# Moving the layer-norm scaling of a four-layer graph network from ScalarE to VectorE, and a rectifier into the copy behind a transpose

## The chip, the cores and the metric

The kernel runs on one core of a Trainium2 chip. The metric is the time of one execution on the device in microseconds (us), as the median of several runs. Everything is computed in float32.

## The reference

Sixty-four batches, each a matrix x of 256 nodes by 128 features, share one adjacency matrix adj (256 x 256). Four layers follow one another, each of the form x = x + f(h), with h the rectified layer norm of x:

```python
h = jnp.maximum(_layernorm(x, axis=-1), 0.0)   # (x - mean) / sqrt(var + 1e-5), before every layer
x = x + layer(h, ...)
# layer 0, W = adj: s1 = h @ adj[:, :128].T, s2 = h @ adj[:, 128:].T
pre = s1[:, :, None, :] + s2[:, None, :, :] + b_lin
h = jnp.where(pre >= 0, pre, ALPHA * pre)       # for all i, j, e
e = jnp.einsum('bije,e->bij', h, a) + bias       # then softmax, attn @ x, sigmoid
# layer 1: dense graph layer with elu, an edge sigmoid and two products
# layer 2: attention with tanh(A / 8) * 8, exp and the adjacency as a mask
# layer 3: five steps of a gated recurrent unit, messages adj @ h
```

Layer 0 holds nearly all of the work: for each batch, 256 x 256 pairs of nodes times 256 values of e go through a leaky rectifier and are summed over e with weights a.

## The kernel before

A turn of the main loop handles a pair of batches; there are 32 pairs and two more turns in which the last pair runs out. A turn has 128 places, called lots, 64 for either batch of the pair. In a lot that is not left out (116 of the 128 from the third turn on, all 128 before it) eight blocks of 128 x 256 values max(u_i, w_j) are made, and TensorE sums them over the partitions into the score bank S with four products (eight records of the trace, L1163). The blocks go into a ring of 12 buffers, so makers can be up to 12 lots ahead of TensorE.

Each block is made by one of three engines. ScalarE does it as a rectifier of a PSUM copy plus a bias (L956, tile ring). GpSimd does it in a tensor-scalar on SBUF (L620). VectorE does it in tensor-tensors of one, two or four blocks (L746, L751), whose w operand lies in PSUM, and in some rows as a max plus a second tile `signed` (L742) that GpSimd makes (L610) and that covers both values of e at once. Which engine gets which block of which lot is settled when the program is built, by the class `Plan`: `stage_costs` books a cost for every other stage of work on its engine near its lot, and `share_blocks` gives the blocks of each lot so that the three running sums of cost stay level. The costs are in units of about 0.1 us: `VECTOR_BLOCK, VECTOR_START, SCALAR_BLOCK, POOL_BLOCK = 2.67, 0.69, 3.57, 4.75`. The stage that makes `src_bias` in layer 1 (L833, four custom instructions on two SBUF operands) is booked as `source=8`.

The other layers run in the same turns, spread over fixed lots by tables: POST is the end of layer 0 of one batch, PRE the layer norm and projections of the next batch (h = 0 or 1), LN1, LN2, LN3 are the norms ahead of layers 1 to 3 of the pair before (four blocks of 128 x 128), L1 and L2 those layers, and L3 the recurrent steps, which go on into the next turn. Every engine runs its own program in order: in each lot first its blocks, then its stages. TensorE does a stage three lots early (LEAD). On VectorE, a stage of several dependent instructions puts one held-back piece of the lot's blocks (`one_piece`) ahead of each wait on its own result; `spare_blocks` says how many pieces are held back.

A layer norm before the change: VectorE takes bn_stats and bn_aggr per block (L802, L808; for PRE L767, L772), then two tiny tensor-scalars, minus_mean (L812, L776) and var + eps (L813, L777). GpSimd raises var to -1/2 (L582) and multiplies minus_mean by it into shift (L584). ScalarE makes the rectified norm with one activation for each block, with scale rstd and bias shift (L1006 for layers 1 to 3, L964 for PRE). TensorE transposes h into PSUM and ScalarE copies it out (L1014, L1041, L1061, L968).

Work on VectorE that reads two SBUF tensors beside GpSimd's: the state update of layer 3 (L890 rh, L894 diff, L898 gated, L902 h3T), the mask products, and L833. In setup_layer0, at the start, L670 multiplies a 128 x 256 SBUF tile by one column in a tensor-scalar.

Of the kernel before, what the change touches and what calls it, by code (L numbers as in the profile page):

```python
# [30 lines left out]
ALU = mybir.AluOpType  # L31
# [3 lines left out]
P = 128  # L35
N = 256
NB = N // P
# [63 lines left out]
class Plan:  # L101
# [45 lines left out]
    def stage_costs(self):  # L147

        vector, scalar, pool = [0.0] * LOTS, [0.0] * LOTS, [0.0] * LOTS

        def put(costs, table, at, **stages):
            for name, cost in stages.items():
                book(costs, at + table[name], cost)

        def book(costs, t, cost):

            costs[t % LOTS] += cost / 2
            costs[(t - AHEAD) % LOTS] += cost / 2

        for h in range(2):  # L160
            half = h * LOTS_B
            if self.turn or h:
                put(vector, POST[h], half, score=7, transpose=1.5, residual=3.4)
                put(scalar, POST[h], half, exp=8, copy=3, tanh=5)
            put(vector, PRE[h], half, stats=7.0)
            put(scalar, PRE[h], half, norm=7.7, copy=2.7, evacuate=32)
            put(pool, PRE[h], half, factors=12)
            if self.has_sums:
                book(pool, half, 11)
        if self.turn:  # L170
            for ln in (LN1, LN2, LN3):
                put(vector, ln, 0, stats=12.5)
                put(scalar, ln, 0, norm=15.4, copy=4.8)
                put(pool, ln, 0, factors=12)
            put(pool, L1, 0, shift=13, halves=13)
            put(vector, L1, 0, elu=10, source=8, mask=12, agg_copy=6, recv_elu=10, residual=6)
            put(scalar, L1, 0, exp=5.7, edge_copy=4.8, tanh=14.2, agg_copy=4.8, recv_exp=5.7)
            put(vector, L2, 0, mask=11.4, residual=11.8)
            put(scalar, L2, 0, copy=9.6, tanh=9.6, exp=9.5)
        for s in range(STEPS):  # L180
            for costs, stages in ((vector, dict(update=7, state=18, out=6 if s == STEPS - 1 else 0)),
                                  (scalar, dict(copy=4.8, reset=5.7, z_gate=5.7, tanh=5.7, back=4.8 if s < STEPS - 1 else 0))):
# [33 lines left out]
    def spare_blocks(self):  # L216

        spare = [0] * LOTS
        for h in range(2):
            for at in (POST[h]["transpose"], PRE[h]["stats"], PRE[h]["stats"]):  # L220
                spare[h * LOTS_B + at] += 1
        for ln in (LN1, LN2, LN3):
            spare[ln["stats"]] += 2
        for at in (L1["elu"], L1["recv_elu"], L2["residual"]):
            spare[at] += 1
        for s in range(STEPS):
            spare[layer3_lot(s, "state")] += 2
        return spare
# [45 lines left out]
def gnn_stack(nc, x, adj, L0_b, L0_a, L1_Wi, L1_bi, L1_We, L1_be, L1_Wn, L1_bn, L1_Wm, L1_bm, L2_q, L2_k, L2_v,  # L274
# [42 lines left out]
    with ExitStack() as ctx:  # L317
# [62 lines left out]
        rstd0 = sb("rstd0", [P, NB])  # L380
        minus_mean0 = sb("minus_mean0", [P, NB])
        shift0 = sb("shift0", [P, NB])
        neg_score = sb("neg_score", [P, NB, N])
# [19 lines left out]
        rstd = sb("rstd", [P, 3, 4])  # L403
        minus_mean = sb("minus_mean", [P, 3, 4])
        shift = sb("shift", [P, 3, 4])
        h1 = sb("h1", [P, 4, P])
# [43 lines left out]

        x_loaded, pre_stats, pre_mv, pre_eps, pre_rstd = (sem(n) for n in "x_loaded pre_stats pre_mv pre_eps pre_rstd".split())
        pre_shift, h0_ready, h0T_psum, h0T_ready = (sem(n) for n in "pre_shift h0_ready h0T_psum h0T_ready".split())
        clamps_ready, signed_ready = sem("clamps_ready"), sem("signed_ready")
# [9 lines left out]
        ln_rstd = [sem(f"ln{n}_rstd") for n in (1, 2, 3)]  # L463
        ln_shift = [sem(f"ln{n}_shift") for n in (1, 2, 3)]
        h_ready = [sem(f"h{n}_ready") for n in (1, 2, 3)]
# [106 lines left out]
        def _(gp):  # L572
# [5 lines left out]

            def factors(var_, minus_mean_, rstd_, shift_, width, sem_in, sem_rstd, sem_shift, value):

                gp.wait_ge(sem_in, value)
                gp.tensor_tensor(rstd_, var_, minus_half[:, 0:width], ALU.pow).then_inc(sem_rstd, 1)  # L582
                gp.wait_ge(sem_rstd, value)
                gp.tensor_tensor(shift_, minus_mean_, rstd_, ALU.mult).then_inc(sem_shift, 1)  # L584

            def pre(value):
                factors(var0[:], minus_mean0[:], rstd0[:], shift0[:], NB, pre_eps, pre_rstd, pre_shift, value)

            def norm(n, turn):
                factors(var[:, n], minus_mean[:, n], rstd[:, n], shift[:, n], 4, ln_eps[n], ln_rstd[n], ln_shift[n], turn.at(1, 0))  # L590

# [64 lines left out]
        def _(dve):  # L656
# [105 lines left out]
            def pre(p, y, value):  # L762

                if p == PRE[1 - y]["stats"]:
# [33 lines left out]

            def stats(t, ln, n, src, pair):
                if t == ln["stats"]:  # L800
# [22 lines left out]
            def layer1(t, turn):  # L823
                pair = turn.at(1, 0)
                if t == LN1["stats"]:
                    dve.wait_ge(x1_ready, turn.at(2, 0))
                stats(t, LN1, 0, X1, pair)
                if t == L1["elu"]:
# [24 lines left out]
            def layer2(t, turn):  # L853
                pair = turn.at(1, 0)
                if t == LN2["stats"]:
                    dve.wait_ge(x2_ready, pair)
                stats(t, LN2, 1, X2, pair)
                if t == L2["mask"]:
# [19 lines left out]
            def layer3(t, turn):  # L878
                if turn.has_l12:
                    if t == LN3["stats"]:  # L880
                        dve.wait_ge(x3_ready, turn.at(1, 0))
                    stats(t, LN3, 2, X3, turn.at(1, 0))
                pair, s, p = layer3_at(turn, t)
# [58 lines left out]
        def _(act):  # L942
# [57 lines left out]

            def norm(t, ln, n, src, dst, pair):

                if t == ln["norm"]:
                    act.wait_ge(ln_shift[n], pair)
                    for r in range(4):
                        last = act.activation(dst[:, r], src[:, r], ACT.Relu, bias=shift[:, n, r:r + 1], scale=rstd[:, n, r:r + 1])  # L1006
                    last.then_inc(h_ready[n], 1)

            def layer1(t, turn):
                pair = turn.at(1, 0)  # L1010
                norm(t, LN1, 0, X1, h1, pair)
# [24 lines left out]
            def layer2(t, turn):  # L1036
                pair = turn.at(1, 0)
                norm(t, LN2, 1, X2, h2, pair)
# [17 lines left out]
            def layer3(t, turn):  # L1056
                if turn.has_l12:
                    norm(t, LN3, 2, X3, h3, turn.at(1, 0))
# [304 lines left out]
```

## Time and profile before

| | |
|---|---|
| median of 3 runs | 5407.69 us (5406.17 to 5408.93) |
| time of the profiled execution | 5412.65 us |
| its span, first to last instruction | 5410.9 us |
| mean granted TensorE clock | 0.996 |
| VectorE busy | 5225.0 us, 97% of the span |
| ScalarE busy | 5143.4 us, 95% |
| GpSimd busy | 5080.7 us, 94% |
| TensorE busy with matmuls | 5288.8 us, 98% |

Busy times are unions of instruction spans, so an instruction that waits inside its span counts as busy. The last 130 us or so are the two turns without layer 0, in which all engines but TensorE are mostly idle.

### The profile page before, as it was taken

The numbers are of one execution on the slowest core, as the hardware profiler recorded it, in microseconds if no ns is written. First come the engines' busy times: TensorE is split into PE (matmuls) and PEld (weight loads), VectorE is DVE, ScalarE is ACT, GpSimd is POOL, SyncE is SP. The second block draws the span as 40 slices with busy tenths as digits, with TensorE's granted clock in tenths as the row PEclk, the third lists the DMA queues.
The fourth block names the chain that finished last, engine by engine and source line by source line (L and its number), as shares of the span: only waits on it lengthen the run. The fifth ranks groups of instructions, "written<-read, shape, count | busy, mean of one in ns | idle before, by whom it ended". The sixth has DMA issues, their size and how long they took to land.

```text
span 5410.9 us, 115261 instructions
## 1 busy us (share of the span) xinstructions
PE 5288.8 (98%) x37702; PEld 2060.9 (38%) x37702; DVE 5225.0 (97%) x10763; ACT 5143.4 (95%) x13517; POOL 5080.7 (94%) x9752
## 2 busy tenths in 40 slices
PE   8999999999999999999999999999999999999997
PEld 2333333333333333333334333333333333333334
DVE  9999999999999999999999999999999999999993
ACT  8999999999999999999999999999999999999993
POOL 8899999999999999999999999999999999999990
PEclk9999999999999999999999999999999999999998
DMA  0000000000000000000000000000000000000000
GB/s 15 3 4 7 7 6 3 6 7 7 6 7 3 6 7 7 6 3 6 7 7 6 7 3 6 7 7 6 3 6 7 7 6 7 3 6 7 7 5 6
DMA packets 44381, 34.00 MB, mean 6 GB/s; under 512 B 4752, under 2 KB 39696, under 8 KB 43792
## 3 DMA queue, kind: packets, MB, share of 16 engines
q1 hardware_dynamic: 43792, 26.63, 1.6%
q8 instruction: 311, 5.10, 0.4%
q14 instruction: 278, 2.28, 0.1%
HBM read 9.84 MB, written 8.39 MB: 3 GB/s over the span
## 4 chain that ended last, share of the span: by engine, by line
PE 52%; ACT 26%; DVE 20%; issue 2%; DMA 0%; POOL 0%; SPq 0%; DVEq 0%; POOLq 0%
PE S L1163 29%; ACT ring L956 20%; PE R L1108 9%; DVE ring L751 8%; PE S L1108 5%; DVE ring L742 4%; PE W L1108 3%; DVE ring L746 2%; PE R L1301 2%; PE V L1108 1%; ACT h L1006 1%; DVE rh L890 1%; DVE gated L898 1%; DVE diff L894 1%; DVE h3T L902 1%
## 5 line engine op out<-in xcount | busy, mean ns | idle before, releaser
L956 ACT ACTIVATE ring<-V,U_minus 128x256 f32<-128x256 f32 x10681 | 4338.4, 850 | 1.6 <-issue 1.6
L1163 PE MATMUL S<-ring,a_window 128*32 128x512 f32 x29888 | 3401.9, 596 | 51.0 <-DVE ring L746 21.4
L620 POOL TENSOR_SCALAR ring<-W,U 128x256 f32<-128x256 f32 x6362 | 3175.7, 518 | 12.1 <-ACT V L982 11.8
L751 DVE TENSOR_TENSOR ring<-U,W 128x512 f32<-128x512 f32 (+1 forms) x2884 | 2536.1, 903 | 7.3 <-ACT V L982 7.3
L1163 PEld LDWEIGHTS S<-ring,a_window 128*32 128x32 f32 x29888 | 886.5, 109 | 2294.5 <-issue 2052.1
L610 POOL TENSOR_SCALAR signed<-W_signed,U_ceiling,U_floor 128x256 f32<-128x256 f32 x2880 | 1699.6, 594 | 6.3
L742 DVE SCALAR_TENSOR_TENSOR ring<-W,U,signed 128x256 f32<-128x256 f32 x2880 | 1193.8, 471 | 0.0
L746 DVE TENSOR_TENSOR ring<-U,W 128x256 f32<-128x256 f32 x1747 | 711.4, 409 | 0.0
L1108 PE MATMUL R<-mT,W 128*128 128x512 f32 (+1 forms) x640 | 334.9, 605 | 16.3 <-ACT mT L1068 16.3
L1108 PE MATMUL R<-AT,h 128*128 128x256 f32 x1264 | 311.9, 390 | 2.1 <-ACT h L1080 2.1
L582 POOL TENSOR_TENSOR rstd<-var,minus_half 128x4 f32<-128x4 f32 (+1 forms) x160 | 144.0, 900 | 141.2 <-DVE var L813 125.6
L1108 PEld LDWEIGHTS R<-AT,h 128*128 128x128 f32 x1264 | 230.6, 193 | 78.4 <-issue 50.3
L890 DVE SCALAR_TENSOR_TENSOR rh<-tr,h3T 128x512 f32<-128x512 f32 (+1 forms) x164 | 165.1, 1007 | 58.3 <-ACT tr L1071 58.3
L1074 ACT ACTIVATE tz<-R,bias 128x512 f32<-128x512 f32 (+1 forms) x160 | 161.1, 1007 | 52.4 <-PE R L1301 52.3
L1006 ACT ACTIVATE h<-X,shift,rstd 128x128 f32<-128x128 f32 x384 | 193.8, 870 | 6.8 <-POOL shift L584 6.8
L1080 ACT ACTIVATE h<-R 128x512 f32<-128x512 f32 (+1 forms) x128 | 131.8, 1029 | 69.5 <-PE R L1309 69.5
L1108 PEld LDWEIGHTS R<-mT,W 128*128 128x128 f32 x640 | 110.5, 192 | 172.0 <-ACT mT L1068 93.7
L1068 ACT ACTIVATE mT<-R 128x512 f32<-128x512 f32 (+1 forms) x160 | 165.0, 1031 | 11.0 <-PE R L1108 11.0
L1301 PE MATMUL R<-mT,W 128*128 128x512 f32 (+1 forms) x320 | 168.5, 608 | 0.0
L1071 ACT ACTIVATE tr<-R,bias 128x512 f32<-128x512 f32 (+1 forms) x160 | 157.6, 985 | 9.6 <-PE R L1108 9.6
L1077 ACT ACTIVATE cand<-R,bias 128x512 f32<-128x512 f32 (+1 forms) x160 | 164.7, 1029 | 0.7 <-PE R L1108 0.7
L1108 PE MATMUL R<-h3T,turned 128*128 128x512 f32 (+1 forms) x320 | 162.6, 590 | 0.0
(185 smaller groups left out, 4512.9 us busy)
## 6 DMA issues: line engine op xcount, KB each, us to landing
X<-in_x SPq DMA_DIRECT2D x64, 128.0 KB, 2.1
X_held<-X SPq DMA_DIRECT2D x32, 256.0 KB, 2.3
out<-OUT SPq DMA_DIRECT2D x64, 128.0 KB, 1.9
edge<-in_L_gnn_w_w SPq DMA_DIRECT2D x3, 128.0 KB, 2.2
A<-in_adj SPq DMA_DIRECT2D x1, 256.0 KB, 2.7
Wn<-in_L_gnn_Wn SPq DMA_DIRECT2D x1, 128.0 KB, 2.9
Wm<-in_L_gnn_Wm SPq DMA_DIRECT2D x1, 128.0 KB, 3.0
weight<-in_L_gnn_u_w SPq DMA_DIRECT2D x2, 64.0 KB, 2.2
```

What stands on the lines that cost most here:

```text
L610: made = gp.tensor_scalar(signed[:, number % 2, at], W_signed[:, y], U_ceiling[:, y, i:i + 1], U_floor[:, y, i:i + 1], ALU.min, ALU.max)
L620: last = gp.tensor_scalar(ring[:, place, g, half * N:(half + 1) * N], W[:, y, c], LARGEST, U[:, y, c, i:i + 1], ALU.min, ALU.max)
L742: piece = dve.scalar_tensor_tensor(ring[:, place, g, half * N:(half + 1) * N], w, U[:, y, c, i:i + 1], signed[:, number % 2, at], ALU.max, ...
L746: piece = dve.tensor_tensor(ring[:, place, g, half * N:(half + 1) * N], U[:, y, c, i:i + 1].to_broadcast([P, N]), w, ALU.max)
L751: piece = dve.tensor_tensor(ring[:, place, g:g + groups].rearrange("p g (h j) -> p g h j", h=NB), u.unsqueeze(3).to_broadcast([P, groups, ...
L890: dve.scalar_tensor_tensor(rh[:, cols_], tr[:, cols_], 1.0, h3T[:, cols_], ALU.add, ALU.mult).then_inc(rh_ready, 1)
L956: last = act.activation(ring[:, place, g, half * N:(half + 1) * N], W_scalar[y][:, c * N:(c + 1) * N], ACT.Relu, bias=U_minus[:, y, c, i:i ...
L1006: last = act.activation(dst[:, r], src[:, r], ACT.Relu, bias=shift[:, n, r:r + 1], scale=rstd[:, n, r:r + 1])
L1068: act.activation(mT[:, cols_], messages[:, cols_], ACT.Copy).then_inc(mT_ready, 1)
L1108: return pe.matmul(dst, lhsT, rhs, start=start, stop=stop)
L1163: last = pe.matmul(S[y][g * ROWS:(g + 1) * ROWS, :], a_window[:, c, ROWS - 1 - row:2 * ROWS - 1 - row], ring[:, place, g], start=False, st ...
L1301: pe.matmul(gates[:, cols_], W345[:, 0], mT[:, cols_], start=False, stop=True, skip_group_check=True).then_inc(z_psum, 1)
```

## The change

VectorE now makes the norm itself: for each 128 x 128 block one tensor-scalar, (x - mean) * rstd, with the mean and rstd as two pointer columns. In PRE (two blocks) and LN3 (four blocks) a second tensor-scalar takes the max with 0 over all blocks at once, behind a wait and a held-back piece. In LN1 and LN2 there is none: the transposes carry signed values, and ScalarE's copy out of PSUM (L1014, L1041) becomes a rectifier. ScalarE's 16 norm activations of a turn go, minus_mean goes from VectorE, the shift product from GpSimd. The norm stands at the same lots as before, on VectorE. The booked costs change, and so the shares of blocks. At the program's start, VectorE waits for rstd and makes the first norm ahead of setup_layer0.

```diff
-            put(vector, PRE[h], half, stats=7.0)
-            put(scalar, PRE[h], half, norm=7.7, copy=2.7, evacuate=32)
-            put(pool, PRE[h], half, factors=12)
+            put(vector, PRE[h], half, stats=6.1, norm=6.6)
+            put(scalar, PRE[h], half, copy=2.7, evacuate=32)
+            put(pool, PRE[h], half, factors=8)
...
-                put(vector, ln, 0, stats=12.5)
-                put(scalar, ln, 0, norm=15.4, copy=4.8)
-                put(pool, ln, 0, factors=12)
+                put(vector, ln, 0, stats=11.3, norm=11.8 if ln is LN3 else 7.9)
+                put(scalar, ln, 0, copy=4.8)
+                put(pool, ln, 0, factors=10)
...
-            for at in (POST[h]["transpose"], PRE[h]["stats"], PRE[h]["stats"]):
+            for at in (POST[h]["transpose"], PRE[h]["stats"], PRE[h]["stats"], PRE[h]["norm"]):
                 spare[h * LOTS_B + at] += 1
         for ln in (LN1, LN2, LN3):
             spare[ln["stats"]] += 2
+        spare[LN3["norm"]] += 1
...
                 gp.tensor_tensor(rstd_, var_, minus_half[:, 0:width], ALU.pow).then_inc(sem_rstd, 1)
-                gp.wait_ge(sem_rstd, value)
-                gp.tensor_tensor(shift_, minus_mean_, rstd_, ALU.mult).then_inc(sem_shift, 1)
...
-                    dve.tensor_scalar(minus_mean0[:], mv0[:, :, 0], -1.0, None, ALU.mult)
                     dve.tensor_scalar(var0[:], mv0[:, :, 1], LN_EPS, None, ALU.add).then_inc(pre_eps, 1)
+                if p == PRE[1 - y]["norm"]:
+                    dve.wait_ge(pre_rstd, value)
+                    for r in range(NB):
+                        last = dve.tensor_scalar(H0[:, y, r], X0[:, y, r], mv0[:, r, 0:1], rstd0[:, r:r + 1], ALU.subtract, ALU.mult)
+                    last.then_inc(pre_scaled, 1)
+                    one_piece()
+                    dve.wait_ge(pre_scaled, value)
+                    dve.tensor_scalar(H0[:, y], H0[:, y], 0.0, None, ALU.max).then_inc(h0_ready, 1)
...
-                    dve.tensor_scalar(minus_mean[:, n], mv[:, n, :, 0], -1.0, None, ALU.mult)
                     dve.tensor_scalar(var[:, n], mv[:, n, :, 1], LN_EPS, None, ALU.add).then_inc(ln_eps[n], 1)
+                if t == ln["norm"]:
+                    dve.wait_ge(ln_rstd[n], pair)
+                    for r in range(4):
+                        last = dve.tensor_scalar(dst[:, r], src[:, r], mv[:, n, r, 0:1], rstd[:, n, r:r + 1], ALU.subtract, ALU.mult)
+                    if n < 2:
+                        last.then_inc(h_ready[n], 1)
+                    else:
+                        last.then_inc(ln3_scaled, 1)
+                        one_piece()
+                        dve.wait_ge(ln3_scaled, pair)
+                        dve.tensor_scalar(dst[:], dst[:], 0.0, None, ALU.max).then_inc(h_ready[n], 1)
...
             dve.memset(minus_half[:], -0.5).then_inc(dve_const, 1)
             pre(PRE[1]["stats"], 0, 1)
+            pre(PRE[1]["norm"], 0, 1)
             setup_layer0()
...
-                if p == PRE[1 - y]["norm"]:
-                    act.wait_ge(pre_shift, value)
-                    for r in range(NB):
-                        last = act.activation(H0[:, y, r], X0[:, y, r], ACT.Relu, bias=shift0[:, r:r + 1], scale=rstd0[:, r:r + 1])
-                    last.then_inc(h0_ready, 1)
...
-                    act.activation(h1T[:], S[1][:], ACT.Copy).then_inc(hT_ready[0], 1)
+                    act.activation(h1T[:], S[1][:], ACT.Relu).then_inc(hT_ready[0], 1)
...
-                    act.activation(h2T[:], W_bank[0][:], ACT.Copy).then_inc(hT_ready[1], 1)
+                    act.activation(h2T[:], W_bank[0][:], ACT.Relu).then_inc(hT_ready[1], 1)
```

## Rows read from the trace of the kernel before

**Rows 1.** The page, its part 1: busy time and share of each engine.

```profile
PE 5288.8 (98%) x37702; PEld 2060.9 (38%) x37702; DVE 5225.0 (97%) x10763; ACT 5143.4 (95%) x13517; POOL 5080.7 (94%) x9752
```

**Rows 2.** Windows: stretch, its length, busy PE, PEld, DVE, ACT, POOL; one steady turn, tail.

```profile
2795.30:2961.00 165.70, 163.55 (x1172) 63.62 (x1171) 163.27 (x337) 160.49 (x425) 160.53 (x307) 1.00 0.02 6
...
5280.00:5411.00 131.00, 94.44 (x334) 62.92 (x334) 44.13 (x114) 46.77 (x94) 7.34 (x8) 0.87 0.02 7
```

**Rows 3.** Chain that ended last, that turn, in order of time: start us, us, what.

```profile
2800.85 0.70 DVE diff L894
...
2835.07 0.36 DVE exp L818
...
2837.76 1.06 PE S L1163 x8
...
2928.48 0.69 ACT tz L1074
...
2931.47 6.56 ACT ring L956 x18
2938.03 1.52 ACT h L1006 x4
```

**Rows 4.** Waits in that turn: who waited for whom, us, times, longest.

```profile
DVE X L850 <- PE S L1108: 1.3, 1, 1.3
...
PE S L1163 <- DVE ring L746: 0.5, 1, 0.5
```

**Rows 5.** Groups by form over the whole span: shapes, count, busy us, mean ns.

```profile
L833 DVE CUSTOM_DVE_ANT_0 exp<-xh,We_src,be 128x128 f32<-128x128 f32 x128 | 71.4, 610 | 2.3 <-ACT xh L1020 2.3
...
L812 DVE TENSOR_SCALAR minus_mean<-mv 128x4 f32<-128x4 f32 x96 | 25.2, 262 | 2.2
```

**Rows 6.** Timeline of the start, VectorE and ScalarE (GpSimd has one short instruction).

```profile
4.93 0.17 DVE L665 TENSOR_SCALAR a_minus<-a_col 128x2 f32<-128x2 f32 x1 [0.68 <-DMA b_col<-in_L_gnn_b_lin]
...
5.48 0.61 DVE L670 TENSOR_SCALAR neg_score<-A,a_abs 128x256 f32<-128x256 f32 x2
...
6.01 0.15 DVE L671 TENSOR_TENSOR b_scaled<-b_col,a_abs 128x2 f32<-128x2 f32 x1
```

**Rows 7.** Timeline of the source stage of layer 1, VectorE and GpSimd, steady turn.

```profile
2844.94 0.70 DVE L833 CUSTOM_DVE_ANT_0 exp<-xh,We_src,be 128x128 f32<-128x128 f32 x1
2845.01 0.49 POOL L620 TENSOR_SCALAR ring<-W,U 128x256 f32<-128x256 f32 x1
...
2847.10 0.87 DVE L742 SCALAR_TENSOR_TENSOR ring<-W,U,signed 128x256 f32<-128x256 f32 x2
```

**Rows 8.** Timeline of the same stage in the tail, first and last of four.

```profile
5299.58 0.35 DVE L833 CUSTOM_DVE_ANT_0 exp<-xh,We_src,be 128x128 f32<-128x128 f32 x1 [2.29 <-ACT xh L1020]
...
5300.67 0.08 DVE L833 DVE_READ_ACCUMULATOR2_ANT src_bias<- 128x1 f32 x1
```

**Rows 9.** Timeline of a layer-3 state update, VectorE and GpSimd, steady turn.

```profile
2801.57 0.91 DVE L898 SCALAR_TENSOR_TENSOR gated<-tz,diff 128x512 f32<-128x512 f32 x1
2801.87 1.03 POOL L610 TENSOR_SCALAR signed<-W_signed,U_ceiling,U_floor 128x256 f32<-128x256 f32 x1
2802.52 0.93 DVE L902 SCALAR_TENSOR_TENSOR h3T<-gated,h3T 128x512 f32<-128x512 f32 x1
...
2834.06 0.68 DVE L902 SCALAR_TENSOR_TENSOR h3T<-gated,h3T 128x512 f32<-128x512 f32 x1
```

**Rows 10.** Timeline around one rh of layer 3, VectorE and GpSimd.

```profile
2822.04 2.74 POOL L620 TENSOR_SCALAR ring<-W,U 128x256 f32<-128x256 f32 x6
2823.37 1.96 DVE L890 SCALAR_TENSOR_TENSOR rh<-tr,h3T 128x512 f32<-128x512 f32 x1
2824.76 1.00 POOL L610 TENSOR_SCALAR signed<-W_signed,U_ceiling,U_floor 128x256 f32<-128x256 f32 x1
```

**Rows 11.** Timeline of the tail: the norm of layer 1 on GpSimd and ScalarE.

```profile
5288.78 0.20 POOL L584 TENSOR_TENSOR shift<-minus_mean,rstd 128x4 f32<-128x4 f32 x1
...
5289.02 1.65 ACT L1006 ACTIVATE h<-X,shift,rstd 128x128 f32<-128x128 f32 x4 [1.60 <-POOL shift L584]
```

More of the change, by code:

```diff
@@ L380, in gnn_stack @@
         rstd0 = sb("rstd0", [P, NB])
-        minus_mean0 = sb("minus_mean0", [P, NB])
-        shift0 = sb("shift0", [P, NB])
         neg_score = sb("neg_score", [P, NB, N])
@@ L403, in gnn_stack @@
         rstd = sb("rstd", [P, 3, 4])
-        minus_mean = sb("minus_mean", [P, 3, 4])
-        shift = sb("shift", [P, 3, 4])
         h1 = sb("h1", [P, 4, P])
@@ L449, in gnn_stack @@
         freed = [sem(f"freed{n}") for n in range(RING)]
-        x_loaded, pre_stats, pre_mv, pre_eps, pre_rstd = (sem(n) for n in "x_loaded pre_stats pre_mv pre_eps pre_rstd".split())
-        pre_shift, h0_ready, h0T_psum, h0T_ready = (sem(n) for n in "pre_shift h0_ready h0T_psum h0T_ready".split())
+        x_loaded, pre_stats, pre_mv, pre_eps, pre_rstd, pre_scaled = (sem(n) for n in "x_loaded pre_stats pre_mv pre_eps pre_rstd pre_scaled".split())
+        h0_ready, h0T_psum, h0T_ready = (sem(n) for n in "h0_ready h0T_psum h0T_ready".split())
         clamps_ready, signed_ready = sem("clamps_ready"), sem("signed_ready")
@@ L463, in gnn_stack @@
         ln_rstd = [sem(f"ln{n}_rstd") for n in (1, 2, 3)]
-        ln_shift = [sem(f"ln{n}_shift") for n in (1, 2, 3)]
+        ln3_scaled = sem("ln3_scaled")
         h_ready = [sem(f"h{n}_ready") for n in (1, 2, 3)]
@@ L577, in _, with factors @@
             gp.wait_ge(dve_const, 1)
-            def factors(var_, minus_mean_, rstd_, shift_, width, sem_in, sem_rstd, sem_shift, value):
+            def factors(var_, rstd_, width, sem_in, sem_rstd, value):
                 gp.wait_ge(sem_in, value)
                 gp.tensor_tensor(rstd_, var_, minus_half[:, 0:width], ALU.pow).then_inc(sem_rstd, 1)
-                gp.wait_ge(sem_rstd, value)
-                gp.tensor_tensor(shift_, minus_mean_, rstd_, ALU.mult).then_inc(sem_shift, 1)
             def pre(value):
-                factors(var0[:], minus_mean0[:], rstd0[:], shift0[:], NB, pre_eps, pre_rstd, pre_shift, value)
+                factors(var0[:], rstd0[:], NB, pre_eps, pre_rstd, value)
             def norm(n, turn):
-                factors(var[:, n], minus_mean[:, n], rstd[:, n], shift[:, n], 4, ln_eps[n], ln_rstd[n], ln_shift[n], turn.at(1, 0))
+                factors(var[:, n], rstd[:, n], 4, ln_eps[n], ln_rstd[n], turn.at(1, 0))
             def blocks(turn, t):
@@ L797, in post, with layer_norm @@
                                              ALU.add).then_inc(x1_ready, 1)
-            def stats(t, ln, n, src, pair):
+            def layer_norm(t, ln, n, src, dst, pair):
                 if t == ln["stats"]:
@@ L826, in layer1 @@
                     dve.wait_ge(x1_ready, turn.at(2, 0))
-                stats(t, LN1, 0, X1, pair)
+                layer_norm(t, LN1, 0, X1, h1, pair)
                 if t == L1["elu"]:
@@ L856, in layer2 @@
                     dve.wait_ge(x2_ready, pair)
-                stats(t, LN2, 1, X2, pair)
+                layer_norm(t, LN2, 1, X2, h2, pair)
                 if t == L2["mask"]:
@@ L881, in layer3 @@
                         dve.wait_ge(x3_ready, turn.at(1, 0))
-                    stats(t, LN3, 2, X3, turn.at(1, 0))
+                    layer_norm(t, LN3, 2, X3, h3, turn.at(1, 0))
                 pair, s, p = layer3_at(turn, t)
@@ L999, in post @@
                     last.then_inc(tanh0_ready, 1)
[L1001 to L1007, printed above, removed]
             def layer1(t, turn):
                 pair = turn.at(1, 0)
-                norm(t, LN1, 0, X1, h1, pair)
                 if t == LN1["copy"]:
                     act.wait_ge(hT_psum[0], pair)
-                    act.activation(h1T[:], S[1][:], ACT.Copy).then_inc(hT_ready[0], 1)
+                    act.activation(h1T[:], S[1][:], ACT.Relu).then_inc(hT_ready[0], 1)
                 if t == L1["exp"]:
@@ L1037, in layer2 @@
                 pair = turn.at(1, 0)
-                norm(t, LN2, 1, X2, h2, pair)
                 if t == LN2["copy"]:
                     act.wait_ge(hT_psum[1], pair)
-                    act.activation(h2T[:], W_bank[0][:], ACT.Copy).then_inc(hT_ready[1], 1)
+                    act.activation(h2T[:], W_bank[0][:], ACT.Relu).then_inc(hT_ready[1], 1)
                 if t == L2["copy"]:
@@ L1057, in layer3 @@
                 if turn.has_l12:
-                    norm(t, LN3, 2, X3, h3, turn.at(1, 0))
                     if t == LN3["copy"]:
```

## The prediction

> **What bounds the kernel now.** I read the page's busy shares first: four engines between 94 and 98% [rows 1], so no single one can be called the bound from there. The windows say the same of one steady turn of 165.70 us: TensorE is idle for 2.15 us of it, VectorE for 2.43, ScalarE for 5.21, GpSimd for 5.17 [rows 2]. The chain that ended last tells which one sets the pace where [rows 3]. From 2800.85, 5.5 us into the turn, it lies on VectorE; at 2837.76 it passes to TensorE, at 2928.48 to ScalarE, and there it stays until the turn ends and VectorE has it again. The reader should see that two of the three stretches belong to the makers of blocks, some 75 us of the turn, and that one of ScalarE's norms (1.52 us for four activations) lies on the chain. Where TensorE has caught up it waits for a late VectorE block, 0.5 us; where it is behind, a stage waits for it, 1.3 us at the residual of layer 1, 78 us into the turn [rows 4]. So a microsecond taken from or given to VectorE between that wait and the next turn's 42 us comes out at the end nearly whole, beyond what slack it has there.
>
> **The change, alone on its engines.** ScalarE loses 16 activations a turn (2 x 2 in PRE, 3 x 4 in the norms) at 0.38 us, 1.52 / 4 [rows 3]: 6.1 us. GpSimd loses five products of 0.20 [rows 11]: 1.0 us. VectorE gets 16 tensor-scalars of 128 x 128. The nearest one is L670, 128 x 256 with one pointer: (6.01 - 5.48) / 2 = 0.265 us from start to start [rows 6]. The 512-wide L818 took 0.36 [rows 3], which is two results a cycle rather than one; with the fixed part of a pointer form, 128 columns less come to 0.265 - 0.067 = 0.20 us. Sixteen are 3.2 us. The maxima over 256 and 512 columns are 2 x 0.21 and 0.34 us, from L818 in the same way. The five minus_means save 0.08 each, 0.4 us (VectorE's other tiny one stays). Three more held-back pieces split a piece each, at 0.69 units or 0.07 us: 0.2. VectorE's own sum is 3.2 + 0.76 - 0.4 + 0.2 = +3.8 us a turn.
>
> The shares of blocks move too. Booked units change by +35.4 on VectorE (2 x 5.7 + 2 x 6.7 + 10.6), -61.6 on ScalarE, -14 on GpSimd, together -40.2, so each engine's booked total falls by 13.4 units, 1.3 us. To get there VectorE hands over 48.8 units of blocks, 4.9 us, nearly all to ScalarE. Without any contention VectorE would end 1.1 us a turn lighter, ScalarE 1.3, GpSimd about 1. The rectifier in L1014 and L1041 replaces a copy of the same size in the same place; with no operand more I cost it at nothing.
>
> **What the shares leave out.** GpSimd reads and writes SBUF 97% of a turn, 160.53 us of 165.70 [rows 2], and some VectorE instructions wait for it. Two such, one behind the other, are L898 and L902: alone 0.68 us, here 0.91 and 0.93, with a GpSimd instruction of 1.03 us slipped in between them [rows 9]; six of its ring blocks take 2.74 us where nothing is in their way [rows 10]. So both sides wait, and they take turns. Block making is outside this: its w operand lies in PSUM. The new tensor-scalars are inside it: they go from SBUF to SBUF, and the tiny L812, a tensor-scalar too, takes 262 ns in the mean where L665 takes 170 with GpSimd out of the way [rows 5, 6]. The best picture of four short ones in a row is L833, also 128 x 128: from the first start to the next instruction 2.16 us in a steady turn, against 1.09 in the tail where GpSimd is idle [rows 7, 8]. That is 0.27 us more each, one GpSimd instruction let in before every one; over the whole run one L833 took 558 ns busy (71.4 / 128) [rows 5]. The planner books this stage at 8 units, 0.8 us, so its numbers don't hold such waits, and norm=7.9 (four at 0.20) doesn't either.
>
> I take 0.27 for each of the 16 new tensor-scalars, 4.3 us, and 0.24 (0.92 - 0.68 [rows 9]) for each of the three maxima, 0.7: 5.0 us a turn. The bounds are nothing for all but the first of a group, if instructions that follow without a wait keep GpSimd out (8 x 0.2 = 1.6 us), and the 1.28 us that one rh lost while GpSimd passed it three times (1.96 against 0.68 [rows 9, 10]) once for each group of tensor-scalars, 6.4 us in place of 1.4. I stay by L833 because it has the same width, the same count and the same neighbour.
>
> The Trainium skill, in SBUF — State Buffer, section Who interferes with whom, says that VectorE in a two-port mode and GpSimd share one port pair as an exclusive lock, held for a whole instruction, and names tensor_scalar among those that take it. This speaks against the change, and the rows on L898 and L902 agree. It also says that whoever issues first gets the pair; by that the rh would have waited 0.5 us, and it waited 1.28, so the measurement leaves room for worse than turn and turn about.
>
> **The sum.** VectorE's work grows by 3.8 - 4.9 + 5.0 = +3.9 us a turn; it had 2.43 us idle [rows 2], so it becomes the slowest engine. Along the chain: between the wait at 78 us and the next turn's 42 us lie LN2, PRE, LN3 and LN1, which is 14 tensor-scalars (3.8 us of waits) and two maxima (0.5). Against it stands the relief that the planner gives in the same stages, (10.7 + 6.0 + 6.8 + 10.7) / 3 = 11.4 units or 1.1 us. Of the 3.2 us left, slack takes some: VectorE isn't on the chain while ScalarE is. I take 0.8 for that, between nothing and the 1.3 of L850's wait [rows 4]. That leaves 2.4 us a turn. ScalarE's relief is worth nothing once VectorE is late.
>
> Thirty steady turns give 72 us, the second turn about 2, the first (PRE alone) 0.5. At the start VectorE now waits for rstd (L584 began at 5.07) and makes a norm before L665, which began at 4.93 [rows 6]: some 0.5 us of work and a wait on it, +1.1 us in all. In the tail GpSimd is idle and the norm chain is shorter: a product of 0.20 and 1.65 us of ScalarE [rows 11] become 0.9 us, three times, of which TensorE's own work hides about a third: -2. Together +74 us on the profiled execution's 5412.65 us, which is 5487. That execution lies 5 us over the median of the runs, so I predict 5482, +1.4%.
>
> **The rivals.** First, other side: instructions issued without a wait between them keep GpSimd out, and each group waits once. For it: L833 has an accumulator read between its instructions and L898 and L902 a semaphore, and no row shows two long plain ones back to back beside a busy GpSimd. Against it: each must ask for the port anew. VectorE then has 3.8 - 4.9 + 1.6 = +0.5 us a turn and its idle time covers it, while ScalarE's stretch, which holds LN3 and one PRE, loses (6.8 + 6.0) / 3 = 4.3 units, 0.4 us. The time is 5408 - 31 x 0.4 - 1 = 5395; this decides if the mean new tensor-scalar steps under about 0.3 us. The Trainium skill's Perfetto Trace Analysis, section Optimizing Scalar/DVE Operations, says an operation with a VectorE performance mode is faster there than on ScalarE; alone, rows give 0.20 against 0.38, and it is the neighbour that undoes it.
>
> Second, no contention at all, only the planner's relief on both stretches: about 1 us a turn, 5408 - 31 - 1 = 5376. L898 and L902 speak against it. Third, groups lose 1.28 us each as the rh did: 5.0 us a turn over my sum, 5482 + 150 = 5632; only one rh a turn shows it, so the mild form, one group a turn, is in the range: +1.3 x 31 = 40 us.
>
> **How the numbers follow.** I give my case 0.65, the first rival 0.25, the second 0.05, the third 0.05. My case alone runs from 5440 (slack of 1.3 us and waits of 0.2 us for a tensor-scalar, 0.9 us a turn) to 5535 (no slack, 5507, and most of a mild third rival). The whole range is 5388 to 5535; it holds the first rival's centre and leaves out the second. A measurement of this kernel can tell about 0.2% from no change, 11 us. Faster takes 0.17 of the first rival and the second: 0.22. Within 0.2%: 0.08 and 0.02 of mine, 0.10. Slower: 0.68.
>
> **What would show it.** Right: the tensor-scalars of 128 x 128 stepping at 0.45 to 0.5 us in steady turns with a GpSimd instruction ending before each, and at 0.2 in the tail; VectorE's busy share at 98%, TensorE's idle time per turn at 4 to 5 us and put down to VectorE blocks; ScalarE idle for more than 7 us a turn; a turn of about 168 us. Wrong: steps of 0.2 to 0.3 us, the chain still on ScalarE at the norm of layer 3's lots, and a turn of 165.3 us. What would upset it most is the slack of VectorE in ScalarE's stretch, which no row gives.

## The result, and the profile after

The kernel with the change takes 5453.41 us in the median of four runs (5450.39 to 5455.51), against 5408.31 for four runs of the kernel before: a ratio of 1.0081 with a 95% interval of 1.0063 to 1.0098. So it is slower, by 45 us where 74 were forecast. The span of the profiled execution grew by 40.9 us, to 5451.8, at the same mean clock (0.996).

The page's busy shares, then the windows of two steady turns in a row (length; busy PE, PEld, DVE, ACT, POOL; granted clock), which answer to [rows 1, 2]:

```profile
PE 5303.1 (97%) x37702; PEld 2041.6 (37%) x37702; DVE 5289.1 (97%) x11224; ACT 5120.0 (94%) x13475; POOL 5062.8 (93%) x9625
```

```profile
2646.20:2813.00 166.80, 163.85 (x1172) 62.95 (x1171) 164.91 (x350) 159.77 (x424) 159.14 (x302) 1.00 0.02 6
2813.00:2980.40 167.40, 164.18 (x1172) 62.79 (x1171) 165.51 (x352) 159.96 (x424) 159.74 (x303) 1.00 0.02 6
```

VectorE has less than 2 us left in a turn (2.43 before), ScalarE and GpSimd have over 7 (5.2 before). Over twenty steady turns the mean turn rises from 165.70 to 167.0 us. The chain's shares on the page say who sets the pace, before (first line) and now (second), and the pieces of the chain in the second of those turns say where, in order of time:

```profile
PE 52%; ACT 26%; DVE 20%; issue 2%; DMA 0%; POOL 0%; SPq 0%; DVEq 0%; POOLq 0%
...
DVE 59%; PE 35%; issue 4%; ACT 2%; POOL 0%; DMA 0%; DVEq 0%; POOLq 0%; SPq 0%
```

```profile
2836.93 1.13 DVE ring L746
2838.07 2.32 DVE h L819 x4
...
2858.33 1.07 PE S L1161 x8
...
2890.90 2.00 PE S L1106 x16
2899.21 1.57 DVE ring L737 x4
...
2914.05 3.39 DVE ring L746 x3
...
2956.37 1.83 DVE h L819 x4
...
2976.64 1.22 DVE ring L746
```

ScalarE's stretch at the end of the turn [rows 3] is gone. The chain leaves TensorE at 2899 and stays on VectorE until the turn is over, but for pieces of "issue" under 1 us, and two groups of new tensor-scalars (L819) are pieces of it, 2.32 and 1.83 us for four.

The groups by form of VectorE: the new scalings of layers 1 to 3 (L819) and of PRE (L775), the maxima (L779, L826), and those that answer to old ones (L846 is L833 of before [rows 5], L903 is L890, whose line of before stands last, by itself):

```profile
L819 DVE TENSOR_SCALAR h<-X,mv,rstd 128x128 f32<-128x128 f32 x384 | 190.4, 556 | 2.3 <-POOL rstd L579 2.3
L903 DVE SCALAR_TENSOR_TENSOR rh<-tr,h3T 128x512 f32<-128x512 f32 x156 | 134.0, 859 | 14.3 <-ACT tr L1069 14.3
L846 DVE CUSTOM_DVE_ANT_0 exp<-xh,We_src,be 128x128 f32<-128x128 f32 x128 | 53.2, 467 | 2.3 <-ACT xh L1020 2.3
L775 DVE TENSOR_SCALAR H<-X,mv,rstd 128x128 f32<-128x128 f32 x128 | 51.2, 443 | 0.9 <-POOL rstd L579 0.9
L779 DVE TENSOR_SCALAR H<-H 128x256 f32<-128x256 f32 x64 | 23.6, 369 | 0.0
...
L826 DVE TENSOR_SCALAR h<-h 128x512 f32<-128x512 f32 x32 | 13.3, 414 | 0.0
```

```profile
L890 DVE SCALAR_TENSOR_TENSOR rh<-tr,h3T 128x512 f32<-128x512 f32 x156 | 161.7, 1037 | 29.9 <-ACT tr L1071 29.9
```

Durations here overlap at their ends, so for a price I go by steps, from one start to the next. The timeline shows them twice. First a group in a steady turn, beside GpSimd; then one in the tail, where GpSimd is idle:

```profile
2733.11 0.47 POOL L615 TENSOR_SCALAR ring<-W,U 128x256 f32<-128x256 f32 x1
2733.29 1.82 DVE L819 TENSOR_SCALAR h<-X,mv,rstd 128x128 f32<-128x128 f32 x4
...
2733.57 0.55 POOL L605 TENSOR_SCALAR signed<-W_signed,U_ceiling,U_floor 128x256 f32<-128x256 f32 x1
...
2735.02 0.68 DVE L746 TENSOR_TENSOR ring<-U,W 128x512 f32<-128x512 f32 x1
```

```profile
5384.74 1.11 DVE L819 TENSOR_SCALAR h<-X,mv,rstd 128x128 f32<-128x128 f32 x4
...
5384.88 1.11 PE L1307 MATMUL R<-ident,h3T 128*128 128x128 f32 x4 [3.35 <-DVE h3T L915]
5385.89 0.43 DVE L826 TENSOR_SCALAR h<-h 128x512 f32<-128x512 f32 x1
```

Alone, the first three steps are 0.255 us each (0.77 between the first and the fourth start, and the last one lasts 0.34: 0.77 + 0.34 = 1.11). Beside GpSimd the four take 1.73 us up to the next start, 0.43 each. Over twenty steady turns the mean step is 0.45 us, 0.48 for the twelve of layers 1 to 3 and 0.36 for the four of PRE. And one group a turn is worse, since GpSimd begins one of its two longest operations, X_shifted, a moment before it:

```profile
2670.56 1.28 POOL L627 TENSOR_TENSOR X_shifted<-X,bm_half 128x512 f32<-128x512 f32 x1
2670.57 2.40 DVE L819 TENSOR_SCALAR h<-X,mv,rstd 128x128 f32<-128x128 f32 x4
...
2671.84 0.61 POOL L605 TENSOR_SCALAR signed<-W_signed,U_ceiling,U_floor 128x256 f32<-128x256 f32 x1
...
2672.89 0.47 DVE L737 SCALAR_TENSOR_TENSOR ring<-W,U,signed 128x256 f32<-128x256 f32 x1
```

GpSimd makes X_shifted in lot 24, right behind LN1's norm in lot 23. The first scaling waits until its 1.28 us are over, once a turn: that scaling lasts 1.36 us in the mean, 0.34 of them its own.

### The profile page after: what moved, and what is told of

Same layout as the page of the kernel before. It is cut to its first block, busy times and chain, and to the rows that moved or that the text cites. A ratio compares the mean times of both kernels' runs of the same rounds, so it can differ in the third digit from the quotient of the medians.

```text
span 5451.8 us, 115553 instructions
## 1 busy us (share of the span) xinstructions
PE 5303.1 (97%) x37702; PEld 2041.6 (37%) x37702; DVE 5289.1 (97%) x11224; ACT 5120.0 (94%) x13475; POOL 5062.8 (93%) x9625
## 4 chain that ended last, share of the span: by engine, by line
DVE 59%; PE 35%; issue 4%; ACT 2%; POOL 0%; DMA 0%; DVEq 0%; POOLq 0%; SPq 0%
DVE ring L746 24%; PE S L1161 19%; DVE ring L737 13%; DVE ring L741 7%; PE R L1106 6%; PE S L1106 4%; DVE h L819 3%; PE W L1106 2%; DVE gated L911 2%; DVE diff L907 2%; DVE h3T L915 1%; DVE rh L903 1%; ACT ring L970 1%; DVE st L805 1%; PE R L1299 1%
## 5 line engine op out<-in xcount | busy, mean ns | idle before, releaser
L970 ACT ACTIVATE ring<-V,U_minus 128x256 f32<-128x256 f32 x11151 | 4415.5, 787 | 1.2 <-issue 1.1
L746 DVE TENSOR_TENSOR ring<-U,W 128x512 f32<-128x512 f32 (+1 forms) x2820 | 2374.1, 867 | 7.3 <-ACT V L991 7.3
L1161 PEld LDWEIGHTS S<-ring,a_window 128*32 128x32 f32 x29888 | 866.9, 109 | 2340.0 <-issue 1922.4
L605 POOL TENSOR_SCALAR signed<-W_signed,U_ceiling,U_floor 128x256 f32<-128x256 f32 x2880 | 1707.6, 596 | 7.1
L741 DVE TENSOR_TENSOR ring<-U,W 128x256 f32<-128x256 f32 x1824 | 746.8, 411 | 0.0
L819 DVE TENSOR_SCALAR h<-X,mv,rstd 128x128 f32<-128x128 f32 x384 | 190.4, 556 | 2.3 <-POOL rstd L579 2.3
L1078 ACT ACTIVATE h<-R 128x512 f32<-128x512 f32 (+1 forms) x128 | 110.5, 863 | 81.5 <-PE R L1307 81.5
L903 DVE SCALAR_TENSOR_TENSOR rh<-tr,h3T 128x512 f32<-128x512 f32 (+1 forms) x164 | 137.4, 838 | 42.8 <-ACT tr L1069 42.8
L1106 PE MATMUL R<-rh,turned 128*128 128x512 f32 (+1 forms) x320 | 161.7, 587 | 0.0
```

Source lines behind the costliest of these rows:

```text
L605: made = gp.tensor_scalar(signed[:, number % 2, at], W_signed[:, y], U_ceiling[:, y, i:i + 1], U_floor[:, y, i:i + 1], ALU.min, ALU.max)
L741: piece = dve.tensor_tensor(ring[:, place, g, half * N:(half + 1) * N], U[:, y, c, i:i + 1].to_broadcast([P, N]), w, ALU.max)
L746: piece = dve.tensor_tensor(ring[:, place, g:g + groups].rearrange("p g (h j) -> p g h j", h=NB), u.unsqueeze(3).to_broadcast([P, groups, ...
L819: last = dve.tensor_scalar(dst[:, r], src[:, r], mv[:, n, r, 0:1], rstd[:, n, r:r + 1], ALU.subtract, ALU.mult)
L903: dve.scalar_tensor_tensor(rh[:, cols_], tr[:, cols_], 1.0, h3T[:, cols_], ALU.add, ALU.mult).then_inc(rh_ready, 1)
L970: last = act.activation(ring[:, place, g, half * N:(half + 1) * N], W_scalar[y][:, c * N:(c + 1) * N], ACT.Relu, bias=U_minus[:, y, c, i:i ...
```

## The experiments

Each ratio is against the kernel before, run beside it on the same chip; its median was 5419.19 us for the first four kernels, 5404.43 for the next four, 5405.41 for the PRE kernel and the one with both small edits, and 5420.04 for the last. "Turn" is the mean of twenty steady turns of the profiled execution, and VectorE's busy time in one is the sum of its steps without its idle time (163.18 us before, 165.08 with the change). The profiled execution is one of four to eleven, and where it is over 0.3% off their median, the text says so.

**The same scalings with an operand in PSUM.** The kernel with the change; each scaling in the loop reads its second factor from a PSUM tile instead of the column rstd. So this kernel leaves out the division by the deviation; it tells what the scalings cost, and is no version to use.

```diff
-last = dve.tensor_scalar(dst[:, r], src[:, r], mv[:, n, r, 0:1], rstd[:, n, r:r + 1], ALU.subtract, ALU.mult)
+last = dve.scalar_tensor_tensor(dst[:, r], src[:, r], mv[:, n, r, 0:1], W_bank[t // LOTS_B][:, 0:P], ALU.subtract, ALU.mult)
```

> The changed kernel, but each scaling multiplies by a 128-column PSUM tile in place of the rstd column (scalar_tensor_tensor), so the layer norms lack their division by the deviation. Alone it costs what the tensor-scalar costs (0.26 us, 16 a turn), the booked shares are the same, and it reads one SBUF tensor only. Theory port (VectorE's SBUF-to-SBUF tensor-scalars and GpSimd take turns): steps of 0.26 instead of 0.45 us, VectorE 3 us a turn lighter, the turn back at 165.2 to 165.9 us, 5390 to 5420 us. Rival work (VectorE has simply more to do, or its order is worse): no change, 5445 to 5460 us.

Measured: 5399.11 us, ratio 0.9965 (0.9953 to 0.9977), turn 165.41. As the port theory had it. Sixteen scalings take 4.13 us a turn in place of 7.19, and VectorE is busy 162.93 us, 2.15 less: of the 3.06 us, 0.9 come back as waits of others, among them the maxima of PRE and L847, the source stage. The groups by form:

```profile
L820 DVE SCALAR_TENSOR_TENSOR h<-X,mv,W 128x128 f32<-128x128 f32 x384 | 106.8, 338 | 2.3 <-POOL rstd L579 2.3
...
L775 DVE SCALAR_TENSOR_TENSOR H<-X,mv,W 128x128 f32<-128x128 f32 x126 | 37.5, 336 | 0.0
```

L820 lasts 338 ns in the mean, as L819 does alone in the tail (0.34): same count, same lots, same shares, same neighbour, no wait. The instruction's form differs too, but that isn't a rival: alone, both forms step at 0.26 us. With the wait gone the rest of the change gains 0.35% over the kernel before. That shows what made it slower.

**The long GpSimd operation moved away.** The kernel with the change, X_shifted six lots later.

```diff
-L1 = dict(shift=24,
+L1 = dict(shift=30,
```

> The changed kernel with GpSimd's X1_shifted (1.28 us) at lot 30 in place of 24, away from the norm of layer 1. Theory port: the first scaling of that norm no longer waits 1.1 us for it, in the stretch in which VectorE sets the pace; the turn loses about 0.9 us, 5420 to 5430 us. Rival work: nothing changes, 5445 to 5460 us, because neither VectorE's nor GpSimd's amount of work does.

Measured: 5533.89 us, ratio 1.0200 (1.0184 to 1.0216); turn 168.84, in a profiled execution that took 5509 us where the other three took 5534. The first scaling of LN1 fell from 1360 to 633 ns as expected, and yet the kernel lost another 1.2%. The timeline around LN2's scaling, the first three of four (one row), and the second of them by itself from a narrower stretch:

```profile
2085.61 3.34 DVE L819 TENSOR_SCALAR h<-X,mv,rstd 128x128 f32<-128x128 f32 x3
...
2086.34 0.55 POOL L605 TENSOR_SCALAR signed<-W_signed,U_ceiling,U_floor 128x256 f32<-128x256 f32 x1
...
2086.87 1.91 POOL L615 TENSOR_SCALAR ring<-W,U 128x256 f32<-128x256 f32 x4
...
2086.35 2.16 DVE L819 TENSOR_SCALAR h<-X,mv,rstd 128x128 f32<-128x128 f32 x1
```

It began at 2086.35, just behind GpSimd's L605 (2086.34), and ended at 2088.51. With some 0.3 us of work of its own it got in at 2088.2 to 2088.3: it let L605 end and then three ring blocks of 0.48 us (1.91 / 4). This scaling took 2083 ns in the mean of all turns, one rh 1578, and VectorE was busy 167.07 us. So a waiting instruction isn't sure of the next gap, and which one is passed over is mostly the same turn after turn, until something moves. Both theories on record had the time wrong.

**The booked costs nearer to the measured ones.** The kernel with the change, and `norm` of PRE, LN1 and LN2, LN3 booked with 10.5, 19.2 and 22.6 units in place of 6.6, 7.9 and 11.8.

> The changed kernel with the norm booked on VectorE at what the trace of the changed kernel shows (PRE 10.5 in place of 6.6, norms of layers 1 and 2 19.2 for 7.9, of layer 3 22.6 for 11.8), so that about 2.7 us a turn of blocks leave VectorE for ScalarE and GpSimd. If the loss is VectorE's load, under-booked by the waits: the turn loses 0.9 to 1.3 us, 5412 to 5425 us. Rival: the loss is in the chain of the layer norm, its latency; then shares don't matter, 5445 to 5460 us.

Measured: 5487.50 us, 5433.94 to 5505.35, ratio 1.0116 (1.0084 to 1.0148). No gain, where one was expected; the interval overlaps that of the change (1.0063 to 1.0098), so it isn't shown to be slower either. The profiled execution was the fastest by far (5433.94, the others 5482 and more; turn 166.62, VectorE busy 163.45), so it doesn't show what the others lost. In it the blocks were handed over as planned, and VectorE's instructions waited 9.1 us a turn over the shortest of their form, against 8.2 with the change. The expectation missed, and its cause stays open.

**The smallest piece: only the shift product.** The kernel before, with minus_mean gone and the product -mean * rstd made on VectorE, in one tiny instruction on two SBUF operands for each norm; GpSimd makes roots only, and its booked costs fall.

```diff
-gp.wait_ge(sem_rstd, value)
-gp.tensor_tensor(shift_, minus_mean_, rstd_, ALU.mult).then_inc(sem_shift, 1)
...
-dve.tensor_scalar(minus_mean[:, n], mv[:, n, :, 0], -1.0, None, ALU.mult)
...
+dve.wait_ge(ln_rstd[n], pair)
+dve.scalar_tensor_tensor(shift[:, n], mv[:, n, :, 0], -1.0, rstd[:, n], ALU.mult, ALU.mult).then_inc(ln_shift[n], 1)
...
-put(pool, PRE[h], half, factors=12)
+put(pool, PRE[h], half, factors=8)
...
-put(pool, ln, 0, factors=12)
+put(pool, ln, 0, factors=10)
```

> The kernel before with one part of the change: GpSimd makes roots only; the tiny product shift is one VectorE instruction in place of minus_mean, the norm stays on ScalarE. GpSimd loses 1.0 us a turn, VectorE gains 0.1 to 0.3 in waits for the port. Theory port and planner: the three balance at 0.2 to 0.3 us a turn less, 5398 to 5406 us. Rival: VectorE now waits for the root and passes it on late, 5408 to 5420 us.

Measured: 5559.32 us, ratio 1.0252 (1.0239 to 1.0265), turn 170.68: three times the loss of the whole change, for five instructions, and far outside both expectations. The five account for 2.6 us a turn; diff rose from 4.0 to 6.5 us a turn. The timeline shows where. A diff has 0.69 us of work; this one ended at 2164.64, so it got in at about 2163.95, behind five ring blocks of some 0.46 us, of which one had just begun as it asked; the sixth had to wait for it:

```profile
2161.61 3.28 POOL L618 TENSOR_SCALAR ring<-W,U 128x256 f32<-128x256 f32 x6
2161.62 3.02 DVE L896 TENSOR_TENSOR diff<-cand,h3T 128x512 f32<-128x512 f32 x1
```

**The same with the shares of the kernel before**, so that GpSimd gets no more blocks (`factors=12` in both places).

> The kernel before with shift made by VectorE and with the booked costs, so the shares of blocks, of before. Theory passing-over (VectorE's small two-input instruction changes at which instant later ones ask for the port, and GpSimd passes some of them over for several instructions): still slower than before, by 0.3 to 2.5%, with single instructions of VectorE over 1.5 us. Rival shares: the 2.5% came from the other distribution of blocks; then 5405 to 5420 us.

Measured: 5445.16 us, ratio 1.0078 (1.0064 to 1.0092), turn 166.73. A third of the loss; diff is back to normal (3.9 us a turn), shift takes 2.34. So most of the 2.5% came with the other shares. The ratio is in the range of the passing-over theory, but its sign isn't there: outside the blocks and the mask product no VectorE instruction of a steady turn lasts over 1.35 us. What is left are short waits, at shift and at the source stage (2.71 us a turn for 2.15 before).

**The parts one by one: layers 1 to 3.** The kernel before, with LN1 to LN3 as in the change, and PRE left on ScalarE.

> Three quarters of the change: the norms of layers 1 to 3 on VectorE (12 scalings a turn and one maximum), PRE left on ScalarE as before. Theory port: these twelve bring 5.8 of the 7.2 us of scalings a turn, so most of the loss: a turn of 166.6 to 167.2 us, 5435 to 5460 us. Rival: it is PRE, whose norm feeds layer 0 of the next half, that is late; then this one is at the time of before, 5400 to 5415 us. A long passing-over of VectorE by GpSimd (1 to 3 us) may add up to 1% to either, and would show as single instructions of over 1.5 us.

Measured: 5500.08 us, ratio 1.0184 (1.0170 to 1.0198), turn 169.12; VectorE busy 167.95 us. That is 40 us and more over what was expected from the scalings alone, and single scalings of 2.17 us are there, as the last sentence of the expectation had it.

**PRE alone.** The kernel before, with PRE as in the change.

> Only the norm of PRE goes to VectorE (4 scalings and 2 maxima a turn), the norms of layers 1 to 3 stay on ScalarE. Port theory in even turns: scalings 4 x 0.45 = 1.8 us, maxima 0.6, less 0.3 for minus_mean and 1.5 of blocks handed over, +0.6 us a turn on VectorE, of which its idle time takes most: ratio 1.000 to 1.004. If the parts of the change add up, PRE would have to make up for what the norms of layers 1 to 3 alone cost (ratio 1.0184 against 1.0081 for both): ratio 0.990. If passing-over decides, it has no fixed sign: up to 1.01, with one VectorE instruction of the turn over 1.2 us in the mean.

Measured: 5404.07 us, ratio 0.9998 (0.9989 to 1.0007), turn 165.48; VectorE busy 163.18 us, as before; the lower end of what the port theory expected. Four scalings cost 1.46 us a turn and two maxima 0.64, and 1.13 of blocks, 0.83 at rh and 0.34 at the source stage come off. The parts don't add: +1.84% and nothing against +0.81% for both. With LN1 to LN3 alone the scalings, the source stage and the X update are all long (first fence); with PRE alone the same two old stages aren't (second):

```profile
L818 DVE TENSOR_SCALAR h<-X,mv,rstd 128x128 f32<-128x128 f32 x384 | 221.8, 638 | 2.3 <-POOL rstd L592 2.3
...
L845 DVE CUSTOM_DVE_ANT_0 exp<-xh,We_src,be 128x128 f32<-128x128 f32 x128 | 89.0, 747 | 3.5 <-ACT xh L1028 3.5
L798 DVE SCALAR_TENSOR_TENSOR X<-tanh,X 128x256 f32<-128x256 f32 x64 | 61.9, 968 | 3.9 <-ACT tanh L1010 3.9
```

```profile
L841 DVE CUSTOM_DVE_ANT_0 exp<-xh,We_src,be 128x128 f32<-128x128 f32 x128 | 59.1, 514 | 2.3 <-ACT xh L1024 2.3
L781 DVE TENSOR_SCALAR H<-X,mv,rstd 128x128 f32<-128x128 f32 x128 | 51.4, 442 | 0.9 <-POOL rstd L588 0.9
L804 DVE SCALAR_TENSOR_TENSOR X<-tanh,X 128x256 f32<-128x256 f32 x64 | 35.3, 552 | 4.6 <-ACT tanh L1002 4.6
```

**Layers 1 to 3 with an operand in PSUM.** The same kernel as for layers 1 to 3, its scalings in the PSUM form, with `ALU.min` as the second operation. Like the first PSUM kernel it leaves out the division. With `ALU.mult`, as there, some values weren't finite, and that version has no time.

> The kernel with only the norms of layers 1 to 3 on VectorE (ratio 1.0184, turn 169.12), with each scaling a scalar_tensor_tensor of the same shape, (x - mean) min a tile of a PUSM bank, in place of times rstd (the division by the deviation is left out). Port theory: scalings 12 x 0.26 = 3.1 us a turn in place of 6.8, and the turn falls to 165.5 us or so, ratio 0.997 to 1.000. If that kernel's loss sits in the other instructions that got slower (the X update 1.8 us, source 2.8), it stays at 1.008 or more.

Measured: 5410.14 us, ratio 0.9984 (0.9975 to 0.9993), turn 165.75. The loss of 1.84% is gone. Twelve scalings take 3.10 us for 6.77, and two of the old groups beside them shrank too (rh didn't: 1028 ns in the mean for 949). Why they did isn't shown, since they come at other lots than the scalings:

```profile
L818 DVE SCALAR_TENSOR_TENSOR h<-X,mv,W 128x128 f32<-128x128 f32 x384 | 106.6, 336 | 2.3 <-POOL rstd L592 2.3
L845 DVE CUSTOM_DVE_ANT_0 exp<-xh,We_src,be 128x128 f32<-128x128 f32 x128 | 60.9, 528 | 3.5 <-ACT xh L1028 3.5
L798 DVE SCALAR_TENSOR_TENSOR X<-tanh,X 128x256 f32<-128x256 f32 x64 | 38.7, 605 | 3.5 <-ACT tanh L1010 3.5
```

**Can the kernel before be made faster?** Three versions: X_shifted six lots later (the edit shown above, on the kernel before); costs booked as its profile has them (`source=20` for 8, `update=9.9` for 7, `state=23.4` for 18, the mask 14.4 for 11.4, exp, copy and tanh of POST 9.8, 6 and 6 for 8, 3 and 5, a ScalarE block 3.65 for 3.57, a GpSimd block 4.55 for 4.75 and a signed tile 5.33 for 5.43, and costs on GpSimd for the time that it waits: mask=10, update=4.5, state=13); and both.

> The kernel before, with GpSimd's X1_shifted at lot 30 in place of 24: no engine's work changes and nobody waits for it. Theory passing-over: the instants at which VectorE and GpSimd meet move, so the time moves by up to 1% in either direction, and the change in VectorE's waits for the port in a turn, summed from the trace, equals the change in VectorE's busy time. Rival: nothing happens, within 0.2% of before, 5397 to 5419 us.

> The kernel before with the stage costs booked as the trace shows them (VectorE's source 20 for 8, layer 3's update and state 9.9 and 23.4 for 7 and 18, GpSimd's losses beside them, blocks at 3.65 and 4.55). VectorE hands over about 1 us a turn. If its load sets the pace: 0.3 to 1 us a turn less, 5375 to 5400 us, and faster than both. If it is where VectorE meets GpSimd that decides, the time goes anywhere within 1%.

> This is the kernel before with both small edits that came out level or a little faster (0.9988 for the measured booked costs, 0.9994 for the later shift). If what they save on VectorE adds up, the ratio is 0.998 and the turn 165.1 us. If which VectorE instructions are passed over by GpSimd is drawn anew with every change of order, the two don't add: the ratio may be anywhere from 0.998 to 1.010, and a new line of VectorE has one mean duration at least 0.8 us over its shortest.

Measured: 5400.86 us, 0.9994 (0.9985 to 1.0003); 5397.11 us, 0.9988 (0.9979 to 0.9996); 5397.16 us, 0.9985 (0.9976 to 0.9994). The later shift left the time within 0.2%, as its rival had it; the booked costs brought 0.28 us a turn, just under what was expected; and both together have a turn of 165.37 us, where a sum would give 165.1. The last is the best complete version, by 0.15%, less than the 0.2% that I called the resolution. Its windows, one steady turn:

```profile
2783.40:2948.77 165.37, 163.69 (x1171) 63.31 (x1170) 160.35 (x321) 160.72 (x425) 160.81 (x306) 1.00 0.02 6
```

VectorE, ScalarE and GpSimd each have 4.6 to 5.0 us to spare, and all of its 27 steady turns last 165.36 to 165.38 us. With that much to spare on the makers of blocks, I read it as the pace of TensorE's order of work, 163.7 us of products and 1.7 us of waits; most turns of the two single edits and over half of PRE alone last 165.37 to 165.39 us too. No run tests it by itself. The kernel before stood 0.33 us above it in its trace, and some 0.27 by the medians (8.25 us over 31 turns). It isn't a hard floor: with its other shares of blocks, about half of the turns of the PSUM kernel of all norms last 165.0 us and others 165.4 to 165.8, two of 28 over 167, with a mean of 165.41.

## Why the prediction was right, and where its size was off

**What bounds.** Right: VectorE became the slowest engine, the chain is 59% on it, and ScalarE's relief is idle time (7.1 us a turn, "more than 7" forecast). TensorE is idle 3.1 us a turn; 4 to 5 were forecast, as a turn of about 168 us was, and it is 167.0. That tensor-scalars would wait was argued from L898 and L902, which read two SBUF tensors each; only the rows of the kernel after and the PSUM kernel show it of tensor-scalars.

**The scalings.** Nearly right in sum, by a different split. A step of 0.47 (0.20 alone and 0.27 of waiting) was forecast, 0.45 measured: 7.19 us for 7.5. Alone it is 0.255, so the size taken over from L670 was too small, and the wait is 0.2. The price came out because the two errors nearly cancel, which is luck. The tail and the two PSUM kernels separate work from wait: 3.06 us of the 7.19 are waits (4.13 are left), and they are more than the 1.6 us by which the turn stands over 165.37.

**The first rival** falls with the steps: instructions without a wait between them don't keep GpSimd out. By its own condition (under 0.3 us) it would have decided at 0.26, and the PSUM kernel is near that world: a ratio of 0.9965 against the 5395 / 5408 = 0.9976 that I gave for it.

**The mis-sized term** is the sum of waits, "5.0 us a turn". I added it to waits of the old instructions taken as fixed. Counted over the shortest duration of each form, for VectorE's instructions with all operands in SBUF and without the statistics, the waits rose from 6.0 to 8.2 us a turn, 2.2. Item by item, predicted and measured, us a turn: scalings 7.5 and 7.19; maxima 1.46 and 0.93 (they wait little: L826 lasts 414 ns beside GpSimd and 0.43 us in the tail, L779 369 ns in the mean and 278 at the shortest); minus_mean -0.4 and -0.70; blocks with their split pieces -4.7 and -4.5; rh nothing and -1.00; the source stage nothing and -0.55; all others nothing and +0.5. Together +3.9 and +1.9. The rh of 1.96 us [rows 10] isn't passed over any more in the kernel after, and L903's mean is 859 ns where L890's was 1037 (both lines stand with the groups above). Why that one got its turn isn't shown, only that such waits are dealt out anew by each change. That the time fell so near the forecast is therefore in part luck: the same pricing gave 166.6 to 167.2 us a turn for layers 1 to 3 alone, which took 169.1, and 5398 to 5406 us for the shift kernel, which took 5559.

**From VectorE to the turn.** Of +3.9 I let 2.4 through; of +1.9 VectorE's idle time took 0.6 and 1.3 came through. Against the 165.37 of the booked kernels it is 1.6, against the 165.0 of the PSUM kernel's best turns 2.0. I had looked for the slack in ScalarE's stretch, between 0 and 1.3 us, and the kernel before had only 0.33 us above that pace; that is also why all relief of makers of blocks (4.5 us of blocks off VectorE, or ScalarE's 6 us) is worth so little.

**The sum, over the run.** Start +1.1 us, as forecast (L660, L665 of before, begins at 5.95 in place of 4.93, and the first X_shifted 1.1 us later). Three first turns -1.0 (+2.5 forecast). The 28 turns after them +38.1, and the last one with blocks +2.3: 40.4, where 70 or so were forecast. Tail +0.4 (-2 forecast): four scalings take 1.11 us rather than 0.9, and LN1's take 2.05, waiting for X_shifted with GpSimd otherwise idle. 1.1 - 1.0 + 40.4 + 0.4 is the 40.9 us of the span.

**The third rival**, long passing-over, is real, though this change drew few of them: 1.6 waits of over 0.65 us a turn and 1.4 us in them (1.0 and 1.2 before), and 1.0 of the 1.4 is the one wait for X_shifted. The kernel with layers 1 to 3 alone drew 3.3 and 3.8 us, the shift kernel 4.0 and 4.8 us. At 0.05 I held it too unlikely; of the seven kernels that gave VectorE more work with SBUF operands alone, three lost more than twice what the change did (2.00, 1.84 and 2.52% for 0.81). A mild form of it was within the range.

## What to carry to other kernels

Before work goes to VectorE in an instruction that reads and writes SBUF, price it beside a busy GpSimd, not alone: 0.45 us a step here for 0.255, more than the 0.38 of ScalarE's activation that it replaced; an operand in PSUM took the wait away (0.26 us a step), where the algorithm has one there. Then expect the old instructions' waits to change too: run the parts singly as well as together, and don't add their results. And look first for the pace of the engine that all others feed: with 5 us a turn free on each maker of blocks it was 0.33 us under the turn of the kernel before, 0.2%, and relief of the others brought no more than that (0.35% in the kernel that leaves work out).

## What the runs showed of the hardware that was not expected

A VectorE instruction that waits for GpSimd isn't always served at the end of GpSimd's current instruction. One scaling (2.16 us long) let four in a row go ahead, one diff (3.02 us) five; in each case only the first had begun before it asked. The Trainium skill, in SBUF — State Buffer, section Who interferes with whom, says that whoever issues first gets the shared ports for the whole instruction, and the other blocks. That agrees with the 1.28 us behind X_shifted. Where both want them at the same moment, the rows show that GpSimd may be next several times over. In twenty steady turns each of the kernel with the change and the one with the shift moved, a waiting VectorE instruction (waits of over 0.2 us) was passed over at about a quarter of the ends of a GpSimd instruction with a ring block next, and at hardly any with a signed tile next. The starts and ends of waits are estimates here, and what decides it isn't shown.

A second pointer column seems to cost time: a 128 x 128 tensor-scalar with two columns steps at 0.255 us with no neighbour, where 0.20 had been worked out from L670 with one. The second operation doesn't explain it: over 512 columns, L831 of the kernel after (two operations with immediates) lasts 0.414 us at the shortest and L826 (one) 0.411. No run varies the columns alone.
